# Tile 1's embedding from three tables, one weight load moved down SP's queue, and new instruction orders and PSUM banks on all engines

## The reference, cut to what matters

```python
h = layernorm(word_emb[ids] + pos_emb[pos] + type_emb[types]) * gamma + beta
h = h + relu(fc(performer_attention(layernorm(h))))       # random features, 44 per head, 16 heads
h = h + low_rank_experts(layernorm(h))                    # 32 prototypes, top 2, rank 16
h = h + causal_rope_attention(layernorm(h))               # 16 heads of 16
h = h + ternary_ffn(layernorm(h))                         # W1, W2 quantised to -1, 0, 1; d_ff 1024
```

## Time and profile before

| | us |
|---|---|
| median of 3 runs (484.67 to 488.57) | 488.35 |
| the profiled execution, as timed | 489.89 |
| its span, first to last instruction | 488.2 |
| PE busy | 396.0 (81%) |
| DVE busy | 366.1 (75%) |
| ACT, POOL busy | 276.7, 246.4 |

### The profile page before, as it was taken

How to read it: one execution, slowest core, us unless ns; L and a number is a source line. 1 busy time by engine, 2 the same in 40 slices (tenths; PEclk the granted TensorE clock), 3 DMA queues, 4 the chain that set the end, 5 groups by cost and what they waited for, 6 DMA issues and landing times.

```text
span 488.2 us, 11666 instructions
## 1 busy us (share of the span) xinstructions
PE 396.0 (81%) x3872; PEld 266.8 (55%) x3901; DVE 366.1 (75%) x1009; ACT 276.7 (57%) x589; POOL 246.4 (50%) x332
## 2 busy tenths in 40 slices
PE   3271757677868798999999988899999998898976
PEld 1140434435555556666666666666666675655634
DVE  4455488989788689889897879688978796765552
ACT  1223565254747385948585858485765747364531
POOL 6854226365747475757675657474654524342000
PEclk9775557589999899999999999999999999999999
DMA  4818614032495556678696989867888665814223
GB/s 113 238 46 247 189 32 88 11 66 54 92 133 106 93 105 130 117 141 150 126 181 105 171 131 148 170 103 117 158 112 153 126 136 97 127 44 77 66 44 77
DMA packets 176860, 56.34 MB, mean 115 GB/s; under 512 B 168416, under 2 KB 174208, under 8 KB 176800
## 3 DMA queue, kind: packets, MB, share of 16 engines
q1 hardware_dynamic: 175216, 51.25, 56.7%
q0 software_dynamic: 1584, 4.33, 3.7%
HBM read 11.85 MB, written 2.36 MB: 29 GB/s over the span
## 4 chain that ended last, share of the span: by engine, by line
PE 32%; issue 13%; DVE 12%; DMA 11%; POOL 6%; ACT 5%; SPq 3%; DVEq 0%; ACTq 0%; POOLq 0%
PE PS L1322 9%; DMA hgT<-hgs 4%; PE PS L1751 3%; PE PS L1885 3%; PE PS L1619 3%; DMA qkT<-qs 3%; PE PS L1384 3%; DMA xTo<-xso 2%; PE PS L1867 2%; DVE split L989 1%; PE PS L1332 1%; DMA rTm<-split 1%; SPq L458 1%; PE PS L1333 1%; PE PS L1493 1%
## 5 line engine op out<-in xcount | busy, mean ns | idle before, releaser
L989 DVE TENSOR_REDUCE split<-PS 128x16 f16<-128x2048 f32 x16 | 36.7, 2297 | 7.9 <-PE PS L1716 7.8
L1332 PE MATMUL PS<-proj_hi,qkT 128*128 128x176 f16 x128 | 24.8, 256 | 18.7 <-DMA qkT<-qs 13.7
L588 POOL TENSOR_TENSOR stage_f<-stage_f 128x512 f32<-128x512 f32 x16 | 20.3, 1269 | 29.0 <-DVE stage_f L977 16.9
L581 POOL TENSOR_TENSOR rstdR<-rstdR,consts 128x1 f32<-128x1 f32 x16 | 8.7, 545 | 51.7 <-DVE rstdR L954 51.7
L1867 PE MATMUL PS<-w1q,xTM 128*128 128x512 f16 x128 | 32.9, 379 | 0.8 <-DVE xTM L1028 0.6
L1885 PE MATMUL PS<-w2q,mT 128*128 128x256 f16 x256 | 30.6, 273 | 1.7 <-ACT mT L1074 0.9
L1619 PE MATMUL PS<-faT_hi,hgT 128*128 128x256 f16 x128 | 26.2, 292 | 5.7 <-DMA hgT<-hgs 5.6
L1077 ACT ACTIVATE ehat<-esum,nmeanE,rstdE 128x256 f32<-128x256 f32 x16 | 9.5, 595 | 37.6 <-DVE nmeanE L770 22.0
L1885 PEld LDWEIGHTS PS<-w2q,mT 128*128 128x128 f16 x256 | 24.3, 98 | 6.0 <-issue 1.9
L1332 PEld LDWEIGHTS PS<-proj_hi,qkT 128*128 128x128 f16 x128 | 13.4, 105 | 24.2 <-DMA qkT<-qs 16.4
L598 POOL TENSOR_TENSOR rstdM<-rstdM,consts 128x1 f32<-128x1 f32 x16 | 8.8, 550 | 33.3 <-DVE rstdM L1016 33.3
(11 more groups left out here) (325 smaller groups left out, 1410.4 us busy)
## 6 DMA issues: line engine op xcount, KB each, us to landing
out<-outb SPq DMA_DIRECT2D x16, 128.0 KB
w<-in_w2T SPq DMA_DIRECT2D x1, 1024.0 KB, 6.2
w<-in_w1T SPq DMA_DIRECT2D x1, 1024.0 KB, 8.6
stage_p<-in_wqkT SPq DMA_DIRECT2D x1, 512.0 KB
stage_f<-in_fbT SPq DMA_DIRECT2D x1, 512.0 KB, 4.8
stage_f<-in_faT SPq DMA_DIRECT2D x1, 512.0 KB, 5.6
stage_r<-in_rwqk SPq DMA_DIRECT2D x1, 512.0 KB, 6.5
rT<-split SPq DMA_TRANSPOSE x26, 3.3
```

Of the source, the lines that this page charges most:

```text
L588: g.tensor_tensor(rot[:, :, :].rearrange("p h d -> p (h d)"), rc[:, :], rs[:, :], ALU.add).then_inc(rot_ok, 1)
L989: v.tensor_reduce(slots(48)[:, 0:H, 0].rearrange("p (c j) -> p j c", j=4), PS[:, BANK["mk1"]:BANK["mk1"] + 4, :].rearrange("p j (c k) -> p ...
L1332: pe.matmul(dst, qkT[:, c0 + c, :], proj_hi[:, :], start=True, stop=False)
```

## The change

Four edits.

1. **Tile 1's embedding.** The gathers of tile 1 are three, as those of tile 0, into a second slot of `emb_type`; the wait for `pt_out` moves to tile 2. In `e2` of tiles 0 and 1 POOL makes two additions instead of one (tile 0 did so before, in another form).
2. **`load_w2`** moves from behind `PT1` to behind `qp0`.
3. **Orders.** `START`, `STRETCH` and `PLACE` are all new, so the lists of all five engines are. BY_PE, WARM and the work of each step stay.
4. **Banks.** `BANK`, `TERN_BANK`, `SET_BANK` are new, and the `free` waits with them.

```diff
+++ after.py
                     sp.dma_start_transpose(xT["P"][:, :, :], xs["P"][:, :]).then_inc(T_ok["P"], 16)
-                    if t == 1:
-                        load_w2()
...
                     sp.dma_start_transpose(qpT[:, :, :], qe[:, :, :].rearrange("p j n -> p (j n)")).then_inc(qp_ok, 16)
+                    if t == 0:
+                        load_w2()
...
-                if t == 1:
+                if t == 2:
                     g.wait_ge(ids_ok, 4)
                     g.wait_ge(pt_out, 16)
...
-                          (emb_type[:, :], A["type"].rearrange("(r n) -> r n", n=D), ids[:, 2, t:t + 1]))
-                if t > 0:
+                          (emb_type[:, t % 2, :], A["type"].rearrange("(r n) -> r n", n=D), ids[:, 2, t:t + 1]))
+                if t > 1:
                     tables = (tables[0], (emb[:, slot, :], A["pt"], ids_pt[:, t:t + 1]))
...
-                    wait(g, g_ok[slot], 32 * (t // RING + 1) + (16 if slot == 0 else 0))
+                    wait(g, g_ok[slot], 32 * (t // RING + 1) + (16 if slot < 2 else 0))
+                    if t < 2:
+                        g.tensor_tensor(h_of(t), h_of(t), emb_type[:, t, :], ALU.add).then_inc(g_const, 1)
+                        wait(g, g_const, 24 + t)
                     wait(g, xn_ok["E"], t)
-                    if t == 0:
-                        g.tensor_tensor(escaled[:, :], h_of(t), emb[:, slot, :], ALU.add).then_inc(g_const, 1)
-                        wait(g, g_const, 24)
-                        g.tensor_tensor(esum[:, :], escaled[:, :], emb_type[:, :], ALU.add).then_inc(e2_ok, 1)
-                    else:
-                        g.tensor_tensor(esum[:, :], h_of(t), emb[:, slot, :], ALU.add).then_inc(e2_ok, 1)
+                    g.tensor_tensor(esum[:, :], h_of(t), emb[:, slot, :], ALU.add).then_inc(e2_ok, 1)
...
-    "qk": 6, "kmxT": 7, "kbc": 7, "fK": 0, "v": 7, "ctx": 2, "fQ": 0, "o": 3,
-    "of": 2, "Ftr": 7, "prt": 1, "fh": 0, "y": 7, "Rtr": 2, "rqk": 2, "rv": 1,
-    "mk1": 3, "pvx": 3, "pvT": 7, "wo": 0, "m1": 4, "m2": 2, "Ptr": 1, "ont": 2,
-    "Mtr": 4, "rot_": 7, "rT3p": 1, "mTp": 3, "rT1p": 0, "rT2p": 4, "hgTp": 6,
+    "qk": 6, "kmxT": 7, "kbc": 7, "fK": 0, "v": 5, "ctx": 7, "fQ": 0, "o": 7,
+    "of": 2, "Ftr": 7, "prt": 0, "fh": 1, "y": 7, "Rtr": 2, "rqk": 2, "rv": 1,
+    "mk1": 3, "pvx": 5, "pvT": 2, "wo": 7, "m1": 3, "m2": 2, "Ptr": 4, "ont": 2,
+    "Mtr": 4, "rot_": 0, "rT3p": 0, "mTp": 4, "rT1p": 6, "rT2p": 0, "hgTp": 0,
```

More of the change, by code:

```diff
@@ L448, in step @@
                     sp.dma_start_transpose(hgT[:, :, :], hgs[:, :]).then_inc(hgT_ok, 16)
+                elif op == "rT1":
+                    wait(sp, rl_ok, t + 1)
+                    wait(sp, rh2_ok, t + 1)
+                    wait(sp, s2_ok, t)
+                    sp.dma_start_transpose(rT[:, 0:HP, :], split[:, 0:H * SLOT]).then_inc(rT1_ok, 16)
                 elif op == "rT2":
@@ L557, in step @@
                     g.tensor_tensor(xs["P"][:, D:], xn["P"][:, :], xs["P"][:, 0:D], ALU.subtract).then_inc(lo_ok["P"], 1)
+                elif op == "onl":
+                    wait(g, hi_ok["o"], t + 1)
+                    g.tensor_tensor(xs["o"][:, D:], onorm[:, :], xs["o"][:, 0:D], ALU.subtract).then_inc(lo_ok["o"], 1)
                 elif op == "qel":
@@ L1155, in step @@
                         setup_f()
+                elif op == "onh":
+                    wait(a, on_ok, t + 1)
+                    wait(a, T_ok["o"], 16 * t)
+                    copy(xs["o"][:, 0:D], onorm[:, :]).then_inc(hi_ok["o"], 1)
                 elif op == "va":
@@ L1159, in step @@
                     a.activation(va[:, :, 0:DH], by_head(PS[:, BANK["v"], 0:D]), ACT.Copy, scale=1.0 / WS).then_inc(va_ok, 1)
+                elif op == "qe2":
+                    wait(a, qd_ok, t + 1)
+                    wait(a, qel_ok, t)
+                    a.activation(qef[:, :], qd[:, :], ACT.Exp).then_inc(qe2_ok, 1)
                 elif op == "qe1":
@@ L1163, in step @@
                     a.activation(qeh[:, :, 0:MP], pairs(qd), ACT.Exp).then_inc(qe1_ok, 1)
-                elif op == "qe2":
-                    wait(a, qd_ok, t + 1)
-                    wait(a, qel_ok, t)
-                    a.activation(qef[:, :], qd[:, :], ACT.Exp).then_inc(qe2_ok, 1)
                 elif op == "ke":
@@ L1299, in step @@
                     copy(xT["M"][:, 0:KC, :].rearrange("p c n -> p (c n)"), PS[:, BANK["Mtr"], 0:D]).then_inc(hi_ok["M"], 1)
+                elif op == "mh2":
+                    wait(a, m1_ok, t + 1)
+                    wait(a, mT_ok, 16 * t)
+                    a.activation(ms[:, 0, 512:1024], PS[:, BANK["m1"] + 1, :], ACT.Relu).then_inc(mh2_ok, 1)
                 elif op == "mh1":
@@ L1500, in step @@
                     free("on_ok", on_ok, t)
-                    free("oh_ok", oh_ok, issued["pvx"])
-                    free("mT_ok", mT_ok, 16 * issued["mTp"])
-                    free("ex1_ok", ex1_ok, issued["mk1"])
+                    free("hR_ok", hR_ok, issued["wo"])
+                    free("kb_ok", kb_ok, issued["kbc"])
+                    free("cth_ok", cth_ok, issued["ctx"])
+                    free("ctl_ok", ctl_ok, issued["ctx"])
+                    free("kmr_ok", kmr_ok, issued["kmxT"])
+                    free("T_F", T_ok["F"], issued["Ftr"])
+                    free("rT1_ok", rT1_ok, 16 * issued["rT1p"])
+                    free("hF_ok", hF_ok, issued["y"])
                     for c, part in enumerate((cth, ctl)):
@@ L1622, in step @@
                     issued["y"] = t + 1
+                elif op == "rT3p":
+                    wait(pe, ngm_ok, t + 1)
+                    wait(pe, rl_ok, t + 1)
+                    wait(pe, rh1_ok, t + 1)
+                    wait(pe, rh2_ok, t + 1)
+                    if t == 0:
+                        pe.wait_ge(v_set, 23)
+                    free("rT3_ok", rT3_ok, 16 * t)
+                    free("kd_ok", kd_ok, issued["fK"])
+                    free("nd2_ok", nd2_ok, issued["prt"])
+                    free("gt_ok", gt_ok, 2 * issued["prt"])
+                    free("hgT_ok", hgT_ok, 16 * issued["hgTp"])
+                    free("qd_ok", qd_ok, issued["fQ"])
+                    free("rT2_ok", rT2_ok, 16 * issued["rT2p"])
+                    free("T_r", T_ok["r"], 16 * issued["rot_"])
+                    free("vr_ok", vr_ok, issued["rv"])
+                    free("hg_ok", hg_ok, issued["fh"])
+                    for c in range(8):
+                        last = pe.transpose(halves_of(BANK["rT3p"] + c // 4)[:, c % 4 * P:(c % 4 + 1) * P],
+                                            split[:, 0:H * SLOT][:, c * P:(c + 1) * P], ident_h[:, :])
+                    last.then_inc(turn_ok, 1)
+                    issued["rT3p"] = t + 1
                 elif op == "Rtr":
                     free("T_R", T_ok["R"], t)
+                    free("ro_ok", ro_ok, issued["pvT"])
+                    free("ob_ok", ob_ok, issued["m2"])
                     free("hP_ok", hP_ok, issued["of"])
                     free("rope_ok", rope_ok, 3 * issued["rqk"])
-                    free("ob_ok", ob_ok, issued["m2"])
-                    free("rT3_ok", rT3_ok, 16 * issued["rT3p"])
-                    free("cth_ok", cth_ok, issued["ctx"])
-                    free("ctl_ok", ctl_ok, issued["ctx"])
                     free("T_o", T_ok["o"], 16 * issued["ont"])
@@ L1651, in step @@
                     issued["rqk"] = t + 1
+                elif op == "rT2p":
+                    wait(pe, rl_ok, t + 1)
+                    wait(pe, rh1_ok, t + 1)
+                    wait(pe, rh3_ok, t + 1)
+                    if t == 0:
+                        pe.wait_ge(v_set, 23)
+                    free("rT2_ok", rT2_ok, 16 * t)
+                    free("T_r", T_ok["r"], 16 * issued["rot_"])
+                    free("rT3_ok", rT3_ok, 16 * issued["rT3p"])
+                    free("kd_ok", kd_ok, issued["fK"])
+                    free("nd2_ok", nd2_ok, issued["prt"])
+                    free("gt_ok", gt_ok, 2 * issued["prt"])
+                    free("hgT_ok", hgT_ok, 16 * issued["hgTp"])
+                    free("qd_ok", qd_ok, issued["fQ"])
+                    free("hg_ok", hg_ok, issued["fh"])
+                    free("vr_ok", vr_ok, issued["rv"])
+                    for c in range(8):
+                        last = pe.transpose(halves_of(BANK["rT2p"] + c // 4)[:, c % 4 * P:(c % 4 + 1) * P],
+                                            split[:, KEYS:KEYS + H * SLOT][:, c * P:(c + 1) * P], ident_h[:, :])
+                    last.then_inc(turn_ok, 1)
+                    issued["rT2p"] = t + 1
                 elif op == "rT1p":
@@ L1746, in step @@
                     free("mT_ok", mT_ok, 16 * issued["mTp"])
[L1747 to L1748 removed]
+                    free("va_ok", va_ok, issued["v"])
+                    free("ex2_ok", ex2_ok, issued["mk1"])
                     for c in range(4):
@@ L1849, in step @@
```

(12 more changed lines are left out.)

467 lines of the change are left out of this document (193 added, 274 removed), and 48 rows, old and new, of the table PLACE.

## The result

| | before | changed |
|---|---|---|
| median (lowest to highest), 21 runs each, one chip | 486.13 us (483.22 to 490.52) | 482.71 us (479.43 to 487.87) |
| the profiled execution, as timed | 489.89 | 482.71 |
| its span | 488.2 | 481.0 |
| ratio of the times, 95% interval | | 0.9915 [0.9894, 0.9937] |

The change makes the kernel 0.85% faster, between 0.63 and 1.06%: 4.1 us of 486. That is inside the 1% which the prediction called "the same". The two profiled spans lie 7.2 us apart. This is more than the change brings, since the profiled execution of before stood 3.8 us above its median of 21 runs. Every ratio in this document is made from fast runs alone; a few executions that were slower or far off are left out.

What follows compares the result with a forecast made beforehand. It took PE to bound the middle (93% busy), DVE 61 to 110, and one tile's chain before 61. Terms 3.9 + 1.5 + 1.0 = 6.4 us, from the median 488.35, gave 482.0 us, range 475 to 491.

Steps and rivals of the forecast that it cites:

- `qT0`, `fQ0`, `qmx0`: First tile: with W2 behind qp0, qT0 lands sooner and qmx0 moves from 47.88 to about 42.1, 5.8 us (lower bound 4.9).
- `PV0` late is hidden: First tile: qk0 starts about 1.6 us late, but qhi0 does not change; bounds -0.3 and +0.6 us.
- W2's landing: First tiles: W2 is there at 57.8, before setup_m would start at about 58.3; 0.5 us left at the worst.
- Not idle for its loads: Sign expected in the new profile: setup_m on ACT does not stand idle for W2 and the biases.
- The order costs 1.4 us: First tiles: qmx1 at about 63.9 though DVE would be free at 62.5, leaving a lead of 3.9 us.
- The lead is carried whole: From 61 to 110 us: the first tiles' lead of 3.9 us is carried to 110 whole.
- the lead is eaten: Rival: the first tiles' lead becomes idle time of DVE or PE before 181; gain 0 to 2, 487 us, chance 0.20.
- 110 to 181: 1.5 us: Stretch 110 to 181: y behind rv and fh mostly removes PE's waits for hgT; gain 1.5 us, bounds 0 and 3.1.
- the middle: 1.0 us: Stretch 181 to 439: fewer waits for hgT against less time for onT before of; net gain 1.0 over 11 rounds.
- `of` waits: Rival, middle: o's new place takes 2.1 us from onT's time, so PE waits; 494 us, 0.13 with other new waits.
- PE's clock stays up early: Rival, 48 to 61 us: shorter idle time keeps PE at full clock, 4.7 us more, 477; 0.12 with a better middle.
- Part 1 outweighs: Rival: the 1.25 us of tile 1's third table is not hidden, sum 483.3; no chance of its own given.

Runs made afterwards that it cites:

- w2_only: Kernel before with only the load of W2 moved from behind PT1 to behind qp0: ratio to before 0.9932 [0.9904, 0.9959].
- w2_back: Changed kernel with the load of W2 put back behind PT1, all else new: ratio to before 1.0013 [0.9986, 1.0040].
- two_tables: Changed kernel with tile 1 gathered from two tables again instead of three: ratio to before 0.9865 [0.9813, 0.9918].
- w2_behind_qT1: Changed kernel with W2 and the biases one step later on SP, behind qT1: ratio to before 1.0059 [1.0027, 1.0092].
- v1_first: Changed kernel with v1 before o0 on PE and qT1 before PT2 on SP: ratio to before 0.9887 [0.9845, 0.9929].
- v1_and_two: Changed kernel with v1 before o0, qT1 before PT2, and tile 1 from two tables: ratio to before 0.9895 [0.9854, 0.9935].
- o_and_ctx_back: Changed kernel with o before v and ctx before fh on PE in the middle tiles: ratio to before 1.0031 [1.0000, 1.0061].
- three_on_old: Kernel before, old orders and banks, with W2 behind qp0 and tile 1 from three tables: ratio to before 0.9938 [0.9914, 0.9962].
- o_before_v: Changed kernel with o put back before v on PE for tiles 3 to 11: ratio to before 1.0145 [1.0112, 1.0178].
- new_pe_on_old: Kernel before with W2 behind qp0 and PE's middle ordered like the changed kernel's: ratio to before 0.9976 [0.9945, 1.0007].
- w2_qT1_first: Kernel before with W2 behind qp0 and qT1 issued before PT2 on SP: ratio to before 0.9919 [0.9891, 0.9947].

## Why the prediction was right, and where it was not

**`qT0`, `fQ0`, `qmx0`.** Forecast: issued at 37.2, landed 40.7, `qmx0` at 42.1. Measured 37.32, 40.48, 41.37. Right, and the mechanism is shown by w2_only and w2_back, which move this one load, in either direction. A part of the way there was set at 0 and wasn't: the wait for `pt_out` that goes gave POOL back 0.4 us.

**`PV0` late is hidden.** `qk0` started at 31.65 and `qhi0` at 34.84, half a microsecond before, just beyond the lower bound (-0.3) of this term. The cover is used up: `qhi0` now waits 0.36 us for `qk0`, and two_tables, with `qhi0` at 33.71 and `qT0` 0.9 us sooner, shows that part 1's delay does pass through. Hidden it is only against the kernel before.

**W2's landing.** Forecast 57.8 with `setup_m` at 58.3; `setup_m` ran at 58.67 after 0.85 us of idle time for the biases, some 9 us after W2 was issued. "Not idle for its loads" was wrong by 0.85 us. It cost nothing, as `qe` behind it still waited 0.81 us for DVE. "Each us beyond that delays ACT" is what w2_behind_qT1 shows.

**"The order costs 1.4 us".** The lead at `qmx1` was forecast 3.9 and was 4.9 in one profile of the changed kernel, 3.4 in the other: the size fits. The cause is half right: `v1` stood at 55.53 and `fQ1` at 61.49, near the 62.5 forecast, but in v1_first an earlier `v1` and `qT1` bring nothing there, as `qT1` then stands behind W2. With W2 1 us sooner as well (v1_and_two) they bring 2.4 us at `qmx1`. Two limits meet at the same place, and the prediction named only one of them.

**The lead is carried whole.** It fits the runs, with 1 to 1.5 us of play: w2_only has 3.7 us at `qmx1` and 3.3 in the time, the changed kernel 3.4 to 4.9 and 4.1, w2_back -1.5 and -0.6. The rival in which the lead is eaten (487, a ratio of 0.997) is outside the interval.

**110 to 181: 1.5 us; the middle: 1.0 us.** These are the terms that failed, 2.5 us together. The waits for `hgT` did go, below 1 us in each stretch, and `xTo` was at 0.7 against a bound of 5. PE was idle 16.6 us of the middle, forecast about 16. All of these signs came true, and the time did not follow. The whole change gained 4.1 us where its lead at `qmx1` was already 3.4 to 4.9, which leaves -0.8 to +0.7 for the two terms, give or take the 1.1 us of the timing; the same reckoning for w2_back leaves 0.9 (above). The prediction counted a wait that goes as time gained. With PE busy 94% and DVE 82% of the middle, PE then waits for `rT`, `xTo` or `xTF`. The reason given for the fall was wrong in part too: it stays with `ctx` back in front of `fh` (o_and_ctx_back), and from 110 to 181 the old lists with W2 moved had 0.6 (w2_only) and 2.0 us (three_on_old) left of the 3.1.

**`of` waits (the rival on the other side).** It did not happen. The price of a badly placed `o` exists, though: 2.2% in o_before_v, through `ctl` and not through `xTo`.

**PE's clock stays up early.** It did not: 0.50 from 48 to 61 in the changed kernel as before, though PE's idle time ahead of it fell from 10.96 to 3.71 us. In the profiles of two_tables, three_on_old and new_pe_on_old it was 0.63 there; their ratios (0.9865, 0.9938, 0.9976) lie on both sides of the changed kernel's.

**Part 1 outweighs.** Unsettled in its small size: 0.3 us on the old lists, 0.5% by the middle values on the new, neither clear of its uncertainty.

**The sum.** Forecast 6.4 us of gain and a time of 482.0; measured 4.1 us by the ratio (3.4 by the medians), and 482.71. The time came out nearer than the gain by luck, from two errors that cancel: the gain was 2.3 us too large, and the median of 3 runs from which it was taken, 488.35, stood 2.2 us above the 486.13 of the 21 runs. The gain that was left is the term of the first tile, 3.9, nearly alone. The outcome called likeliest, a gain clear of the 1% line (0.56), did not come; the measured 0.85% lies in "the same", which had 0.35.

## What to carry to other kernels

Before anything else, look in a queue for the small transfer on the chain that stands behind a bulk load; here its move into a gap took 3.9 us off the small transfer's landing and 3.3 us off the time, and the next place behind the gap cost 6.8 us. A wait that disappears from a full pipeline's list is not time gained until a run with this edit alone says so. An order on one engine has its price in the lists of the others: one step moved back on PE alone, to the place that the kernel before gives it, cost 2.2%. And a lead of a few us in one profile is not a finding until the same kernel has been profiled twice; here two profiles of one kernel differed by 1.5 us at `qmx1`.

## What the runs showed of the hardware

- A transposition of 128 x 512 fp16 (`qT0`) was there 3.2 us after its issue with no bulk load in front, 7.0 us with 1.3 MB right in front of it. `qT1`, issued 2.6, 2.9 and 3.1 us behind W2, was there after 7.7, 7.4 and 9.1 us (w2_qT1_first, v1_and_two, v1_first).
- W2 and the biases, 1.3 MB, were there 9.1 us after W2's issue in the changed kernel (49.55 to 58.67), 10.3 us in two_tables (49.16 to 59.41) and 7.8 us in w2_behind_qT1 (60.38 to 68.20).
- Chips of the same kind gave medians of 482.66 to 486.33 us for the kernel before, a spread of 0.8%, as large as the effect under study.
